# Order of the attention scores on TensorE, and one bias add on another engine, in a two-layer transformer kernel

## What is computed

```python
x = norm(x + attention0(x))    # 16 heads of 8 features, full softmax
x = norm(x + butterfly_ffn(x)) # gelu(x @ Wup + bhid) @ Wdown, hidden width 512
x = norm(x + attention1(x))    # low-rank projections, rope, causal softmax
x = norm(x + gated_ffn(x))     # (silu(x @ Wg) * (x @ Wu)) @ Wd, hidden width 384
# attention, for each head: s = q k^T / sqrt(8); p = exp(s - max s) / sum; o = p v
```

## Time and profile before

| | |
|---|---|
| median of three runs | 333.36 us |
| the profiled execution's own time | 331.46 us |
| its span, first to last instruction | 329.7 us |
| TensorE busy | 281.9 us, 85% |
| VectorE busy | 263.6 us, 80% |
| ScalarE busy | 207.4 us, 63% |
| GpSimd busy | 205.6 us, 62% |
| mean granted TensorE clock | 0.955 |

### The profile page before, as it was taken

How to read it: one execution, slowest core, us unless ns; L and a number is a source line. 1 busy time by engine, 2 the same in 40 slices (tenths; PEclk the granted TensorE clock), 3 DMA queues, 4 the chain that set the end, 5 groups by cost and what they waited for, 6 DMA issues and landing times.

```text
span 329.7 us, 9464 instructions
## 1 busy us (share of the span) xinstructions
PE 281.9 (85%) x3194; PEld 199.3 (60%) x3194; DVE 263.6 (80%) x1007; ACT 207.4 (63%) x428; POOL 205.6 (62%) x326
## 2 busy tenths in 40 slices
PE   7989989997989989888997887988898888898763
PEld 3667555654666446554675456766676666666553
DVE  4897887879588888899679697687899999965565
ACT  2576865776857668496986569666385757536110
POOL 0549994471348447583779785697769756457332
PEclk9999969999899999999999799997799999899978
DMA  6684250303030220404022130403114040000000
GB/s 229 251 248 158 81 195 3 129 0 129 3 112 18 61 101 18 145 8 139 18 64 99 33 130 6 136 23 99 65 27 153 1 146 4 19 2 17 18 16 32
DMA packets 20495, 25.84 MB, mean 78 GB/s; under 512 B 3744, under 2 KB 14304, under 8 KB 20320
## 3 DMA queue, kind: packets, MB, share of 16 engines
q1 hardware_dynamic: 20016, 24.72, 22.4%
q10 hardware_dynamic: 432, 0.53, 0.5%
HBM read 6.36 MB, written 1.05 MB: 22 GB/s over the span
## 4 chain that ended last, share of the span: by engine, by line
PE 42%; DVE 32%; issue 12%; ACT 7%; POOL 4%; DMA 1%; POOLq 0%; ACTq 0%; DVEq 0%
PE bank L600 13%; DVE mx L824 7%; DVE room_c L832 6%; PE bank L615 4%; PE bank L398 4%; PE bank L388 4%; ACT E L728 3%; PE bank L465 3%; DVE turned L923 2%; PE bank L482 2%; DVE room_a L893 2%; DVE room_c L858 2%; PE bank L556 2%; PE bank L567 2%; DVE mx L832 2%
## 5 line engine op out<-in xcount | busy, mean ns | idle before, releaser
L728 ACT ACTIVATE E<-bank 128x512 f32<-128x512 f32 (+1 forms) x256 | 120.3, 550 | 78.4 <-PE bank L411 41.5
L824 DVE TENSOR_REDUCE mx<-bank 128x2 f32<-128x512 f32 x128 | 78.9, 679 | 9.3 <-PE bank L388 9.2
L832 DVE CUSTOM_DVE_ANT_0 room_c<-bank,mask_sb 128x256 f32<-128x256 f32 (+1 forms) x256 | 72.7, 349 | 1.3 <-PE bank L388 1.1
L398 PE MATMUL bank<-QK 32*128 32x256 f32 x480 | 55.8, 316 | 18.5 <-DVE hid L860 6.8
L388 PE MATMUL bank<-QK 32*128 32x256 f32 x480 | 56.8, 313 | 8.1 <-DVE mx L832 2.6
L600 PE MATMUL bank<-E,V 128*32 128x256 f32 (+1 forms) x1024 | 60.7, 383 | 0.1
L398 PEld LDWEIGHTS bank<-QK 32*128 32x128 f32 x480 | 36.9, 188 | 29.3 <-issue 21.8
L388 PEld LDWEIGHTS bank<-QK 32*128 32x128 f32 x480 | 37.2, 187 | 23.3 <-issue 8.9
L1052 POOL TENSOR_SCALAR_AFFINE_SELECT E<-E 128x512 f32<-128x512 f32 x64 | 39.2, 638 | 11.4 <-ACT E L728 11.3
L600 PEld LDWEIGHTS bank<-E,V 128*32 128x32 f32 x1024 | 31.5, 117 | 23.5 <-issue 7.0
L923 DVE STREAM_TRANSPOSE turned<-bank 128x256 f32<-128x256 f32 x32 | 14.3, 446 | 21.8 <-PE bank L600 21.8
(11 more groups left out here) (127 smaller groups left out, 558.7 us busy)
## 6 DMA issues: line engine op xcount, KB each, us to landing
spread_qk<-parts SPq DMA_DIRECT2D x30, 256.0 KB, 2.5
spread_qk<-parts SPq DMA_DIRECT2D x60, 128.0 KB, 2.1
room_c<-room_c SPq DMA_DIRECT2D x64, 32.0 KB, 1.9
xb<-x_nat SPq DMA_DIRECT2D x1, 1024.0 KB, 6.9
out<-ln_g SPq DMA_DIRECT2D x7, 128.0 KB, 1.9
xt<-x_t SPq DMA_DIRECT2D x1, 768.0 KB, 6.7
wi<-wi_all SPq DMA_DIRECT2D x1, 576.0 KB, 4.4
room_c<-fac_u SPq DMA_DIRECT2D x1, 508.0 KB, 6.5
```

The source lines that it names most:

```text
L398: nc.tensor.matmul(g_bank["exp", m][:, c * T:(c + 1) * T - q0], both[:, 1, c * P:(c + 1) * P], both[:, 0, q0:T], start=(c == 0), stop=False)
L728: act.activation(E[:, a % E_RING, j, 0:n], g_bank["exp", m][:, 0:n], ACT.Exp, scale=SCALE)\
L824: ins = nc.vector.tensor_reduce(mx[:, n % 2, :, i], bank[:, :].rearrange("p (q k) -> p q k", q=QT), AX.X, ALU.max, negate=True)
L832: ins = nc.vector.tensor_tensor_reduce(out=masked_s[:, at % 2, lo:hi], in0=bank[:, lo:hi], in1=mask_sb[:, T + lo - hi:T], scale=-1.0, scal ...
```

## The change

Two edits. In TensorE's program, the first call keeps its order, but waits for the turned maxima only ahead of the subtraction; in the second call the two maxima come first, wait for their own two banks only, and the exponentials' banks are waited for behind them, with both exponentials' products after both maxima's. The number of products is the same. And the 16 bias adds of layer 0's way up go from VectorE to ScalarE, into the same steps, behind the copies of projections and transposes.

```diff
-            def scores(maxima, exps, at):
-
-                for i, m in enumerate(maxima):
-                    take((at + i) % BANKS, ("max", m), A["max_done"], order_of(m))
-                for i, m in enumerate(exps):
-                    take((at + len(maxima) + i) % BANKS, ("exp", m), A["exp_done"], m + 1)
+            def banks_for_maxima(maxima, i):
+                for m in maxima:
+                    take(i % BANKS, ("max", m), A["max_done"], order_of(m))
+                    i += 1
...
+            def banks_for_exps(exps, i):
                 for m in exps:
-                    if m % 8 == 0:
-                        pe.wait_ge(A["mt_ready"], m // 8 + 1)
-
-                first = exps and exps[0] % QUAD == 2
+                    take(i % BANKS, ("exp", m), A["exp_done"], m + 1)
+                    i += 1
...
+            def step_scores(g, at):
+
+
+                ahead = range(g + LEAD, g + LEAD + QUAD)
+                banks_for_maxima(ahead[2:], at)
+                banks_for_exps((g, g + 1), at + 2)
                 for long in range(2):
-                    for m in exps if first else ():
+                    for m in ahead[2:]:
+                        max_scores(m, 1 - long)
+                    for m in (g, g + 1):
                         exp_scores(m, long)
-                    for m in maxima:
-                        max_scores(m, 1 - long)
-                    for m in () if first else exps:
+                if g % 8 == 0:
+                    pe.wait_ge(A["mt_ready"], g // 8 + 1)
+                for m in (g, g + 1):
+                    less_maximum(m)
+                banks_for_maxima(ahead[:2], at + QUAD)
+                for c in (1, 0):
+                    for m in ahead[:2]:
+                        max_scores(m, c)
+                banks_for_exps((g + 2, g + 3), at + QUAD + 2)
+                for c in range(2):
+                    for m in (g + 2, g + 3):
+                        exp_scores(m, c)
+                for m in (g + 2, g + 3):
+                    less_maximum(m)
...
                 if g + LEAD < HEADS:
-                    scores((g + LEAD + 2, g + LEAD + 3), (g, g + 1), at)
-                    scores((g + LEAD, g + LEAD + 1), (g + 2, g + 3), at + QUAD)
+                    step_scores(g, at)
                 elif g < HEADS:
-                    scores((), range(g, g + QUAD), 0)
+                    last_scores(g)
...
@@ -744,6 +776,14 @@
+                for c in range(HC):
+                    if (n := tile_at(g, AT_UP0[c])) is not None:
+                        if n == 0 and c == 0:
+                            act.wait_ge(bhid_ready, 1)
+                        if n and c == 0:
+                            act.wait_ge(F0["down_ps"], 2 * n)
+                        act.wait_ge(F0["up_ps"], HC * n + c + 1)
+                        act.activation(hid0[:, c, :], g_bank["up0", n, c][:, :], ACT.Identity, bias=bhid[:, c:c + 1]).then_inc(F0["pre_ready"], 1)
@@ -883,15 +923,6 @@
-                for c in range(HC):
-                    if (n := tile_at(g, AT_UP0[c])) is not None:
-                        if n == 0 and c == 0:
-                            dve.wait_ge(bhid_ready, 1)
-                        if n and c == 0:
-                            dve.wait_ge(F0["down_ps"], 2 * n)
-                        dve.wait_ge(F0["up_ps"], HC * n + c + 1)
-                        nc.vector.tensor_scalar(hid0[:, c, :], g_bank["up0", n, c][:, :], bhid[:, c:c + 1], None, ALU.add)\
-                            .then_inc(F0["pre_ready"], 1)
```

More of the change, by code:

```diff
@@ L428, in scores, with maxima_at_first, last_scores @@
                         pe.wait_ge(A["qk_ready"], 2 * (b - 1) + m % H // 8 + 1)
+            def banks_for_exps(exps, i):
                 for m in exps:
-                    if m % 8 == 0:
-                        pe.wait_ge(A["mt_ready"], m // 8 + 1)
-                first = exps and exps[0] % QUAD == 2
+                    take(i % BANKS, ("exp", m), A["exp_done"], m + 1)
+                    i += 1
+            def maxima_at_first(maxima, at):
+                banks_for_maxima(maxima, at)
+                for c in (1, 0):
+                    for m in maxima:
+                        max_scores(m, c)
[3 more added lines that the diff above has]
+                banks_for_exps((g, g + 1), at + 2)
                 for long in range(2):
-                    for m in exps if first else ():
+                    for m in ahead[2:]:
+                        max_scores(m, 1 - long)
+                    for m in (g, g + 1):
                         exp_scores(m, long)
-                    for m in maxima:
-                        max_scores(m, 1 - long)
-                    for m in () if first else exps:
+                if g % 8 == 0:
[3 more added lines that the diff above has]
+                banks_for_maxima(ahead[:2], at + QUAD)
+                for c in (1, 0):
+                    for m in ahead[:2]:
+                        max_scores(m, c)
+                banks_for_exps((g + 2, g + 3), at + QUAD + 2)
[4 more added lines that the diff above has]
+                    less_maximum(m)
+            def last_scores(g):
+                banks_for_exps(range(g, g + QUAD), 0)
+                if g % 8 == 0:
+                    pe.wait_ge(A["mt_ready"], g // 8 + 1)
+                for long in range(2):
+                    for m in range(g, g + QUAD):
                         exp_scores(m, long)
-                for m in exps:
+                for m in range(g, g + QUAD):
                     less_maximum(m)
@@ L500, in _ @@
             project(1, take(6, ("qk", 1), A["qk_out"], 2))
-            scores((2, 3), (), 0)
-            scores((0, 1), (), 2)
+            maxima_at_first((2, 3), 0)
+            maxima_at_first((0, 1), 2)
             project_group(1, 7)
             project_group(2, 0)
-            scores((6, 7), (), 4)
-            scores((4, 5), (), 6)
+            maxima_at_first((6, 7), 4)
+            maxima_at_first((4, 5), 6)
             project_group(3, 1)
             project_values(0, take(3, ("v", 0), A["v_ready"], 1))
-            scores((10, 11), (), 4)
-            scores((8, 9), (), 6)
+            maxima_at_first((10, 11), 4)
+            maxima_at_first((8, 9), 6)
             turn_maxima(0, take(2, ("mt", 0), A["mt_ready"], 1))
```

## The result

The changed kernel took 327.48 us (median of 20 runs, 323.68 to 329.88), the kernel before, beside it on the same chip, 331.86 us (20 runs, 328.09 to 336.25). The ratio is 0.9866, with a 95% interval of 0.9832 to 0.9899: 1.3% faster, some 4.4 us. The three runs from which the forecast started (median 333.36) are the first of these 20 and lay 1.5 us above their median.

A forecast was written before the change was run, and what follows sets the result against it. It saw no single bound: TensorE and VectorE hand over inside each step, VectorE without slack in layer 1 and the second tile's way up. Terms -3.5 + 0.8 - 0.4 = -3.1 us from 333.36 gave 330.3 us, range 327.8 to 333.5.

The forecast's parts named there:

- The bias adds, 3.5 us: Layer 0's way up: moving 16 adds to ScalarE lets claims start sooner; 0.6 + 1.35 + 0.6 + 0.9 us by tile.
- 0.6 to 1.4: Sign of being right: first claim of steps 60, 92, 124 and 156 sooner by this many us after the first call.
- The second call's order, +0.8 us: Maxima ahead of exponentials in TensorE's second call: 0.11 us lost in each of about 7 steps around the layer change.
- eight products in two rounds become eight in three: Second call: exponentials no longer run in the maxima's shadow, costing TensorE 0.11 us in a step with no wait.
- the new waits inside a call cost something only if unmet; I take nothing: Second call: satisfied waits already stand between claims with no gap, so the new ones were put at no cost.
- the list of steps: About 7 of 61 steps, ahead of and around the layer change, where TensorE alone was said to set the pace.
- The wait for the turned maxima, -0.4: First call: later wait gains a quarter of the 1.7 us idle in four steps; bounds 0 and 1.7 us.
- The strips: Rival: TensorE sets the pace in most steps, so the new order costs up to 6.7 us; 336.2 us, chance 0.13.
- No difference: Rival: gain returns as ScalarE's lateness or in layer-change chains, or order costs some 3 us; about 332.9 us, chance 0.22.
- VectorE as the bound altogether: Rival: the removed 9.2 us of VectorE adds come off in full, 324 us; over 5 us gained has chance 0.1.
- The maxima's scores come sooner, and nobody takes them sooner: Second call: VectorE takes its four maxima in one run and never waits for the second pair, so nothing is gained.
- Theory C: Follow-up theory, not in the prediction: the new second-call order costs a little but raises the mean granted clock, by 0.008.

The follow-up runs named there:

- the adds alone: Kernel before with only the 16 bias adds moved to ScalarE, scores' order as it was; 328.07 us, ratio 0.9965.
- the order alone: Changed kernel with the bias adds back on VectorE; 329.11 us, ratio 0.9918, and a second time 331.14 us, ratio 0.9961.
- 12 adds on ScalarE: Changed kernel with the first two adds of the first and third tile left on VectorE; 327.88 us, ratio 0.9868.
- the two kernels with the long cast: Changed kernel with first-call products also put apart, 327.19 us; changed kernel with second-call products interleaved and exponentials' banks claimed between, 326.44 us.
- the mixed kernel: Changed kernel with old second call in steps 40, 56, 80, 120, 152 and 12 adds on ScalarE; 326.59 us, again 327.38 us.
- The two last kernels: Changed kernel with second-call products interleaved, exponentials' banks claimed between, 326.44 us; changed kernel with all four banks claimed first, 330.28 us.

## Why the prediction was wrong in its number and where it was right

The direction and the order of size held: forecast -3.1 us, measured -3.54 at equal clock, -4.4 as timed. By its own steps:

**The starting point** is what put the time outside the range. "From the median, 333.36 - 3.1": the median of three runs was 1.5 us above that of 20, and the range, built from the terms of the change alone, left no room for it. From 331.86 the same sum gives 328.8, and a range moved down by the same 1.5 us holds the 327.48.

**The bias adds, 3.5 us:** right in mechanism, short in size. 1.21 us for the second tile (1.35 said), 0.90 for the first (0.6), 0.54 for the third with its loss of 0.25 (0.6, with 0.2), 1.13 for the fourth (0.9): 3.8 us, and 0.31 from the stall in step 136, which nothing in the rows of before foretold. Together 4.1 by steps, 4.74 +- 0.6 at equal clock. The claims came sooner by 0.91, 0.91 and 0.79 us in steps 60, 92 and 124 and 1.16 in step 156 (1.26 with the adds alone), within "0.6 to 1.4". ScalarE's adds cost 701 ns, not 690. The extra gain in the first tile: its maxima start at 1.25 us into step 60, as in the second tile, not 1.55, and the loss of 0.3 us said for its first half was 0.03.

**The second call's order, +0.8 us:** "eight products in two rounds become eight in three" failed as a mechanism. Putting products apart costs 0.01 to 0.02 us. What cost 0.10 to 0.17 was the term that the sum put at nothing: "the new waits inside a call cost something only if unmet; I take nothing". They were met, and cost it. The size, 0.11 in a step without a wait, was right by luck (the second call ends at 1.42 us in step 208 instead of 1.31), the list of steps nearly so: 40, 80 and 152 by 0.17, 56 by 0.18 where the adds are on ScalarE too, and 0.3 us in steps 0 to 20, which the list did not have.

That it costs nothing in layer 1 was right and for the reason given, VectorE: the period of 16 heads (steps 208 to 220) is 16.71 us before, 16.70 and 16.68 with the order alone and 16.68 with 12 adds on ScalarE (17.27 in the two kernels with the long cast). By these steps that is 0.7 us with the adds on VectorE, where 152 is paid back, and 1.0 with them on ScalarE. At equal clock the order costs 0.1 +- 0.5 (its first 12 runs -0.1, its second +0.4) with the adds on VectorE, the later wait included, and 1.4 with them on ScalarE; the steps account for 0.3 us of that difference, and the rest is not explained.

The prediction weighed the Trainium skill's "TensorEngine Tiling (Array Packing)", Key Properties: tiles run loads and matmuls in parallel. The rows agree, and more fully than I read them: 0.02 us from first to first, though four products are issued ahead. It was my step from "parallel" to "only if issued in turn" that had no row behind it.

**The wait for the turned maxima, -0.4:** 0.3 +- 0.5 at equal clock, and 0.6 us by the lengths of steps 0 to 20; its bounds held it.

**The rivals.** The strips (336.2 us): excluded, layer 1's steps 208 and 212 are 3.75 + 4.65 against 3.65 + 4.76. No difference: excluded by the interval. VectorE as the bound altogether (324 us): no, 9.2 us would have come off and 4.1 did. "The maxima's scores come sooner, and nobody takes them sooner" was right in the steps without a wait.

**What the prediction has no word for** is the clock, worth 1 us here and 9 between two runs of the kernel before.

## What to carry to other kernels

When an engine's work is moved, count the gain at the claims that stood behind it and the loss at the engine that takes it, half by half: here half of the moves earned nearly all, and two pairs cost. Two waits, though met, in the middle of a group of parallel matmuls cost 0.1 us and more, the order of the matmuls nothing; and where the wait was unmet, running other matmuls ahead of it gained nothing, since the path went from the release through the exponentials. When one step of a pipeline gets longer and the next one shorter by as much, look for the engine that sets the time of both before calling the second a gain. And compare kernels at equal granted clock and step by step before believing a per cent: the ratios alone gave the gain to the wrong half of the change.

## What the runs showed of the hardware

**The clock.** In every trace TensorE's clock falls from its full level (2.4 GHz) to half (1.2 GHz) in a handful of stretches. One of them in the changed kernel, in step 212, with what lies ahead of it and behind it, from two answers of the windows (length, busy times, then the clock, 1.00 or 0.50):

```profile
252.70:256.10 3.40, 2.61 (x35) 2.24 (x33) 3.23 (x16) 2.22 (x7) 1.88 (x5) 1.00 0.00 0
256.20:259.40 3.20, 3.20 (x41) 1.78 (x42) 2.03 (x13) 1.85 (x4) 3.01 (x6) 0.50 0.03 8
259.60:263.00 3.40, 3.33 (x36) 2.85 (x36) 3.32 (x20) 2.44 (x7) 2.63 (x5) 1.00 0.63 231
```

Ahead of the fall TensorE was busy 2.61 of 3.40 us (it waited there for an exponential's bank), inside it all of the 3.20 us. The trace before had eight such stretches, the changed one nine, the order alone five and six, and no kernel more than eleven. Two executions of one kernel can have them in the same places: the mixed kernel's two profiled ones have the same slices, the changed kernel's two differ in one, the order alone's two in four. But these pairs have nearly the same mean clock, and over its 20 runs the changed kernel's goes from 0.939 to 0.975, so they are not always there. The mixed kernel, first and second:

```profile
PEclk9999989999999999999996999989999977899958
```

```profile
PEclk9999989999999999999996999989999977899958
```

A stretch is worth about a microsecond: step 212 took 5.68 us in the changed kernel, where the clock fell, and 4.64 to 4.85 where it didn't. Whether moving a step by 0.2 us moves a stretch was not tried by itself.

**Late claims and the clock.** The nine sets of runs with the exponentials' claims behind the maxima's products (80 runs) have mean clocks of 0.950 to 0.960, averaging 0.954; the seven with all claims ahead (145 runs) 0.945 to 0.953, averaging 0.948. The two last kernels fell on the side of their claims (0.957 and 0.946), not of their order of products. The difference, 0.006 +- 0.003, is worth about 1.3 us and makes up for what the claims cost, which is why the changed kernel, the one with the old second call, and that with the new call in most steps lie within a microsecond in their medians. Why the claims should do this was not tried, the ranges of the two groups overlap, and the kernel before alone went from 0.945 to 0.952 from set to set. Theory C, said ahead of the runs, missed its clock in five of them (0.955 where 0.958 or more was expected, 0.950 and 0.951 for 0.952, 0.954 for 0.957, 0.950 for 0.943 to 0.949). It is a lean of the data and not a cause shown.
